# A cross-attention layer on one core: a new order of steps on all engines, values projected straight into the layout of the direct passes, and finer signals

## What is computed

```python
xn = _ln(x, ln1_w, ln1_b);  sx = _token_shift(xn, state[:, i1])
xxx = jnp.tanh((xn + sx * maa_x) @ maa_w1).reshape(b, l, 5, 1, EXTRA_MAA)
xxx = jnp.matmul(xxx, maa_w2).reshape(b, l, 5, E)
x5 = xn[:, :, None] + sx[:, :, None] * (maa_stack + xxx)          # five mixes
w = jnp.exp(-jnp.exp(time_decay + jnp.tanh(x5[:, :, 1] @ decay_w1) @ decay_w2))
r = x5[:, :, 3] @ Wr.T;  k = x5[:, :, 0] @ Wk.T;  v = x5[:, :, 2] @ Wv.T
g = jax.nn.silu(x5[:, :, 4] @ Wg.T)
def step(s, rkvw):                                                # scan over tokens, per head
    a = k_t[:, :, :, None] * v_t[:, :, None, :]
    out = jnp.einsum('bhk,bhkd->bhd', r_t, u * a + s)
    return (a + w_t[:, :, :, None] * s, out)
x = x + (head_norm(att) * gn_w + gn_b) * g @ Wo.T
xn2 = _ln(x, ln2_w, ln2_b);  sx2 = _token_shift(xn2, state[:, i0])
x = x + sigmoid(xr @ ffn_Wr.T) * (square(relu(xk @ ffn_Wk.T)) @ ffn_Wv.T)
```

## Time and profile before

| | us |
|---|---|
| median of 3 runs | 796.24 |
| the runs | 795.71, 796.24, 813.81 |
| span of the profiled execution | 793.8 |

### The profile page before, as it was taken

The page is one execution under the profiler, slowest core; times in us unless marked ns, Lnnn a source line. Parts: engine busy times, 40 slices in busy tenths (PEclk is TensorE's granted clock), DMA queues, the critical chain, the costliest instruction groups (busy, mean ns, idle before and its releaser), DMA issues.

```text
span 793.8 us, 17668 instructions
## 1 busy us (share of the span) xinstructions
PE 705.9 (89%) x7412; PEld 491.4 (62%) x7412; DVE 513.6 (65%) x767; ACT 324.7 (41%) x639; POOL 376.7 (47%) x223
## 2 busy tenths in 40 slices
PE   5986899997999889998799979998799978998797
PEld 4763677465674667556664665746665556755673
DVE  5638865695567774597556966677736965479441
...
DMA packets 19275, 28.79 MB, mean 36 GB/s; under 512 B 5888, under 2 KB 11776, under 8 KB 18176
## 3 DMA queue, kind: packets, MB, share of 16 engines
...
...
## 4 chain that ended last, share of the span: by engine, by line
PE 51%; issue 15%; POOL 14%; DVE 11%; ACT 7%; DMA 0%; POOLq 0%; DVEq 0%; ACTq 0%
PE FB L563 17%; PE BAB L820 7%; POOL pp L488 7%; PE FA L838 5%; PE FB L571 5%; PE FA L872 2%; ACT half L1048 2%; PE BAB L797 2%; PE FA L639 2%; DVE kvs L1357 2%; PE BAB L555 2%; PE FA L859 2%; PE BAB L733 2%; POOL mixes L453 2%; POOL mixes L451 1%
## 5 line engine op out<-in xcount | busy, mean ns | idle before, releaser
L488 POOL TENSOR_TENSOR pp<-rT,kT 128x2048 f32<-128x2048 f32 (+1 forms) x32 | 108.6, 3406 | 51.7 <-DVE rT L1229 51.7
L451 POOL TENSOR_TENSOR mixes<-mixes 128x1024 f32<-128x1024 f32 x30 | 72.0, 2400 | 127.9 <-ACT mixes L971 127.9
L453 POOL TENSOR_TENSOR mixes<-mixes,xnT 128x1024 f32<-128x1024 f32 x30 | 71.8, 2392 | 2.4
L563 PE MATMUL FB<-mixes,wk_s 128*128 128x256 f32 x256 | 66.1, 417 | 5.8 <-POOL mixes L453 3.5
L1321 DVE TENSOR_REDUCE half<-half 128x256 f32<-128x2048 f32 (+2 forms) x32 | 64.4, 2014 | 0.6
L504 POOL TENSOR_TENSOR acc<-acc,half 128x512 f32<-128x512 f32 x32 | 41.1, 1283 | 49.5 <-DVE half L1321 48.3
L563 PE MATMUL FB<-mixes,wv_s 128*128 128x256 f32 x256 | 60.8, 382 | 2.5 <-issue 1.5
L563 PE MATMUL FB<-mixes,wg_s 128*128 128x256 f32 x256 | 62.1, 392 | 0.0
L563 PEld LDWEIGHTS FB<-mixes,wk_s 128*128 128x128 f32 x256 | 52.1, 208 | 15.9 <-POOL mixes L453 4.5
L971 ACT ACTIVATE mixes<-FA,cols_s 128x256 f32<-128x256 f32 x116 | 45.4, 481 | 38.4 <-PE FA L639 33.4
L838 PE MATMUL FA<-wide,fk_s 128*128 128x256 f32 x256 | 57.2, 381 | 3.5 <-DVE wide L1472 2.2
...
## 6 DMA issues: line engine op xcount, KB each, us to landing
...
vp<-vT SPq DMA_DIRECT2D x128, 32.0 KB, 1.9
...
```

What stands on the lines that cost most here:

```text
L451: nc.gpsimd.tensor_tensor(slot, slot, sx, ALU.mult).then_inc(s_["mixm_ready"], 1)
L453: nc.gpsimd.tensor_tensor(slot, slot, xnT[:, :, 1:L + 1], ALU.add).then_inc(s_["mix_ready"], 1)
L488: ins = nc.gpsimd.tensor_tensor(pp[:, i % 2, 0:size].rearrange("p (n i j) -> p n i j", i=m, j=m), spread(r.unsqueeze(3), 3, m), spread(k.u ...
L563: ins = nc.tensor.matmul(dst[:, c * L:(c + 1) * L], weight[:, q, c * P:(c + 1) * P], src[:, q, :], start=(q == 0), stop=(q == C - 1))
```

## The change

1. **Order.** All lists of `ORDER` are new, and the pass without an `n_` step (front of 7, back of 6, tail of 5) gets a list of its own, `end`. The warm steps of the last pass are gone; `c_fv0` and `c_fv1` stand later there.
2. **Values.** `vT`, `prime` and its DMAs are gone. The centred weight `wv` is stored with its columns permuted (`f_centre`), so that the projection lands in grouped layout, and ACT copies it to `vp`. `b_vtok` turns `vp` with a strided output.
3. **Front banks.** `f_norm` waits for the first `c_mul` alone (in pass `end` for `relu` only), `c_fv1` now waits until ACT has read the norm from `FA` (`xnT_ready`), and `f_m20` waits for the second `c_mul`.
4. **Signals.** `f_norm`, `b_gn` and `b_norm2` signal their bank by halves; `ru_ready` comes before r is copied; `keys_ready` lets `b_ktok` start before the last decay of r; `kvfree_ready` lets `b_acc` start before DVE has added; `f_dec1` takes its mix by halves; `b_step` forms the totals before it waits for POOL.

```diff
@@ ORDER, tensor, last @@
-            c_fk b_score0 c_fr0 b_score1 c_fr1 b_g0 b_score2 b_g1 b_g2 b_score3 b_g3 c_fv0 b_score4 b_vtok c_fv1
-            b_ktok b_kv0 b_kv1 warm14 b_acc b_apply0 b_apply1 b_apply2 b_apply3 warm8 warm20 b_gn0 b_gn1 b_wo0
-            b_wo1 warm22 b_norm20 b_norm21 warm12""".split()),
+            c_fk b_score0 c_fr0 b_score1 c_fr1 b_g0 b_score2 b_g1 b_g2 b_score3 b_g3 b_score4 b_vtok b_ktok
+            b_kv0 b_kv1 c_fv0 b_acc b_apply0 b_apply1 b_apply2 b_apply3 c_fv1 b_gn0 b_gn1 b_wo0 b_wo1 b_norm20
+            b_norm21""".split()),
@@ walk @@
-            run(None, at(B - 1), at(B - 2), at(B - 3))
+            run(None, at(B - 1), at(B - 2), at(B - 3), order["end"])
@@ sync @@
-            def prime(b):
-
-                sp.wait_ge(s_["v_ready"], 2 * b + 2)
-                for c in range(C):
-                    for g in range(NG):
-                        sp.dma_start(vp[32 * c:32 * c + 32, g * L:(g + 1) * L], vT[32 * g:32 * g + 32, c * L:(c + 1) * L]
-                                     ).then_inc(s_["vp_ready"], 16)
@@ gpsimd @@
-                        pool.wait_ge(s_["r_ready"], 2 * b + 2)
+                        pool.wait_ge(s_["ru_ready"], 2 * b + 2)
@@ tensor @@
+            def transpose_grouped(dst, src):
+
+                eye = ident_s[:, :].rearrange("p (c i) -> p c i", c=C)
+                for t in range(T):
+                    for g in range(NG):
+                        to = dst[:, t * E:(t + 1) * E].rearrange("p (c g i) -> p g c i", c=C, g=NG)[:, g]
+                        ins = nc.tensor.transpose(to, src[:, g * L + t * P:g * L + (t + 1) * P], eye)
+                return ins
...
-                if not first(b):
-                    pe.wait_ge(s_["mixe_ready"], NMIX * b)
-                    pe.wait_ge(s_["mul_ready"], T * (b - 1))
-                transpose_channels(FA, xhat).then_inc(s_["xhatT_ready"], 1)
+                if isinstance(b, int) and b == 1:
+                    pe.wait_ge(s_["mixe_ready"], NMIX)
+                elif last(b):
+                    pe.wait_ge(s_["relu_ready"], 2 * b - 2)
+                elif not first(b):
+                    pe.wait_ge(s_["mul_ready"], T * b - 3)
+                transpose_channels(FA, xhat, range(T), s_["xhatT_ready"])
...
-                pe.wait_ge(s_["step_ready"], 4 * b + 4)
+                pe.wait_ge(s_["keys_ready"], b + 1)
...
-                pe.wait_ge(s_["kvs_ready"], b + 1)
+                pe.wait_ge(s_["kvfree_ready"], T * b + T)
...
+                        if q == 0 and not (isinstance(b, int) and b >= B - 2) and (t == 1 or isinstance(b, int) and b == B - 3):
+                            pe.wait_ge(s_["xnT_ready"], b + 3)
@@ scalar @@
-                act.wait_ge(s_["nrmT_ready"], T * b + T)
                 for c in range(C):
+                    act.wait_ge(s_["nrmT_ready"], 2 * b + 1 + c // 2)
...
-                copy = f_proj("projv_ready", vT, "v_ready", "q4_ready", 1, i)
+                copy = f_proj("projv_ready", vp, "v_ready", "q4_ready", 1, i)
@@ vector @@
-                        dve.wait_ge(s_["vp_ready"], 16 * NG * NG * (b + 1))
+                        dve.wait_ge(s_["v_ready"], 2 * b + 2)
...
             def f_centre(b, par, n):
-                centre(w_loaded["wv"], big["wv"][:, :, :].rearrange("p q (h s) -> p (q h) s", s=S),
-                       gT[:, 0:C * H], s_["vmean_ready"], s_["vcen_ready"])
+                mean = gT[:, 0:C * H]
+                centre(w_loaded["wv"], wv_raw.rearrange("p (h s) -> p h s", s=S), mean, s_["vmean_ready"])
+                nc.vector.tensor_scalar(mean, mean, 1.0 / S, None, ALU.mult).then_inc(s_["vmean_ready"], 1)
+                dve.wait_ge(s_["vmean_ready"], 2)
+                for q in range(C):
+                    own = slice(q * E, (q + 1) * E)
+                    ins = nc.vector.tensor_tensor(
+                        big["wv"][:, q, :].rearrange("p (g c h s) -> p c g h s", g=NG, c=C, s=S),
+                        wv_raw[:, own].rearrange("p (c g h s) -> p c g h s", c=C, g=NG, s=S),
+                        spread(mean[:, q * H:(q + 1) * H].rearrange("p (c g h) -> p c g h", c=C, g=NG).unsqueeze(4), 4, S),
+                        ALU.subtract)
+                ins.then_inc(s_["vcen_ready"], 1)
```

177 lines of the change are left out of this document (103 added, 74 removed).

## The result

The changed kernel takes **790.32 us** (median of 7 runs, 787.83 to 794.18) beside 797.5 us for the kernel before (7 runs, 795.71 to 813.81). The ratio is 0.993, 95% interval 0.991 to 0.995; the run of 813.81 us was in a slower state of the chip and is left out of it. The forecast was 770, with a range that began at 757 and ended at 790. So the kernel is faster, but by 0.7% and not by 3.3%, and the question is where the other 20 us went.

A forecast was written before the change was run, and what follows sets the result against it. Bound: PE's own queue and the back's chain, about equally late. Gains 17.0 (main passes) + 3.5 + 0 + 0.8 + 1.5 + 3.0 = 25.8 from 793.8 give 768.0; with 2.4 around the span, 770 us, range 757 to 790.

The forecast's parts named there:

- Start, to `f_lora0`: Main pass from `c_fk`: no new wait on the path, so `f_lora0` begins at 35.7 us, before 36.6.
- ACT takes it back: Main pass behind `f_lora0`: ACT's queue cuts the 0.9 us head start to 0.4; `f_k0` begins at 51.5.
- rival 3: PE falls to half clock in last pass and tail without warm steps: 776 us, or 779 with second pass; 14%.
- It just holds: Main pass: states are spread by 59.3 to 60.6 us, before the last apply at 60.8; applies end at 61.5.
- Root, late end: Main pass, applies to head norm: 5.2 or 7.2 us; the late end starts the norm at 68.7, pass 89.0.
- the pass of 87.0: Main pass takes 87.0 us, not 89.0, if the scan loses 1.9 wherever no POOL mix runs beside it.
- Pass `end`, 3.5: The pass before the last takes 89.6 us where it took 93.1: 3.5 won, bounds 0 to 6.
- Values 0: Removing the values' DMAs gains 0, since they landed before their first reader and cost nothing on the path.
- first and second pass (0.8 and 1.5): Gains of 0.8 us in the first pass (earlier first score) and 1.5 in the second (new order of scores).
- Last pass and tail, 3.0: Removing warm blocks wins 3.0 us there; bounds 6.6 won and 3 lost, with slow starts of 2.5 in two places.
- Rival 1: A new wait replaces the old ones in main passes, each winning only 1 us: 787 us; 20%.
- Rival 2: ACT's queue becomes the bound; a main pass takes 94.3 us, 11 lost, 807 in all; 6%.

The follow-up runs named there:

- e5: Changed kernel plus short strings of idle TensorE matmuls: 8 ahead of `f_m21`, 7 ahead of `b_gn0` in main passes, others in second and last pass; 773.99 us, ratio 0.971.
- e9: e5 with its 15 idle matmuls of a main pass cut from 128 columns to 4, same number and places; 782.24 us, ratio 0.978.
- e4: Changed kernel with POOL's `f_mix3` held until DVE's root is complete, in the main passes and pass `end`; 789.26 us, ratio 0.991.
- e13: e5 with the 7 idle matmuls ahead of `b_gn0` cut to 4 columns, the 8 ahead of `f_m21` whole; 774.66 us, ratio 0.972.
- e7: Changed kernel with POOL's `f_mix3` waiting for DVE's gate product in the main passes and `f_mix4` behind both `b_wo`; 783.2 us, ratio 0.986.
- e3: Changed kernel's code (values, signals) with all lists of steps of the kernel before; 795.59 us, ratio 0.998.
- e11: e5 without idle matmuls in the second pass and with the kernel before's lists in first and second pass; 776.56 us, ratio 0.974.
- e12: e7 plus idle TensorE matmuls, 8 ahead of `f_m21`, 2 ahead of `b_gn0`, and those of the last pass; 784.0 us, ratio 0.981.

## Why the prediction was wrong, point by point

- *The 2.4 us around the span.* 1.8 to 1.9 in every run that has both numbers; the 2.4 set the span of one run against the median of others.
- *Start, to `f_lora0`.* Right: 35.9 against 35.7, and 35.9 to 36.1 in every run with the new main list.
- *"ACT takes it back ... `f_k0` 51.5", and "PE waits here some 4 us in all".* The queue was right: at full clock (e5) `f_k0` begins at 51.2. **This is the step that failed, in what it left out.** I placed the waits and then priced every matmul behind them by rows at full clock. With 2.15 us of them in one piece the clock fell; `f_k0` came at 52.8. The prediction names it as what would make it wrong ("if the clock falls in the main passes, where the waits at `f_m21` to `f_k0` lie close together"), but gave it no price in the sum and no chance: rival 3 had the half clock in the last pass only. The main passes fell 16.3 us short of the sum (0.7 for 17.0): 13.0 by the clock (e9 against e5), 4.7 between the changed kernel and e9, of which some 2 are its pauses and the rest is open, less 1.4 by which the sum was too careful (443.8 and not 445.2).
- *Applies, "It just holds".* It holds, 61.6 in e5. Its terms add up to 58.3 to 60.1, not to 59.3 to 60.6; in the pass from 507.65 the spreading ended at 60.4 on DVE and 60.5 on ACT. The pauses, two of them, were in no term. Rows of before had them, with 7.8 us in three main passes, so the 92.4 that I subtracted from was itself not clean: its two passes without a pause took 91.9 and 91.8. Between clean passes the order gains 3.0 us, near the 3.4 of the sum.
- *Root, late end.* Right: 7.8 from the applies to `b_gn`, forecast 7.9. The stall of 2.2 moved to a later instruction, as the late end assumed; taking it out is worth 1.3 a pass by e4 and not 2.
- *`b_gn` to `wo` 2.8.* 3.9 measured, 2.8 in e5: the clock again.
- *The scan, and the pass of 87.0.* The prediction has 87.0 if the scan loses its 1.9 us. It lost them in all eight batches (2.29 us and not 4.15), with no mix of POOL beside it, and the pass was not shorter for it. The mix had moved to the spreading that follows, 5.87 us where it was 3.81, which has no term in the sum.
- *Pass `end`, 3.5.* 1.4 in the profiled run, 3.0 at full clock with a pause of 2.27 in it (e13), 5.1 in e7 with neither. The size was inside its bounds, 0 to 6.
- *Values 0.* Not contradicted: e3 has them and the signals together at 0.998 (0.995 to 1.002). The prices of first and second pass (0.8 and 1.5) had the wrong sign: `c_fk` came at 134.9 and 134.8 with the old lists (e3, e11), at 136.0 to 138.2 with the new ones (141.8 in e12), and at 138.0 to 141.9 where fillers stand in the second pass. Behind `wo` the new second list has `f_k3`, `f_m24`, `f_v2` and `f_v3` to do, 19.4 us to `c_fk` where it was 18.2. I had given that list its earlier scores and not counted what it puts behind `wo`. That is 1.2 of the 3.4; the other 2.2 are there when `wo` begins (118.8 and not 116.6), 0.8 of them at DVE's first product (52.03 and not 51.21), and no run looked for their cause.
- *Last pass and tail, 3.0.* 2.8, and the price of the missing warm matmuls is visible: `wo` took 8.52 us (7.11 before) behind a wait of 1.06, and `c_fk` 9.86 (7.07 before) behind one of 1.84. That is 4.2 together, near the 2.5 in each of two places, for which no row stood. With that price the low end is 6.6 - 5.0, so 1.6 won; the bound of 3 lost has no working. With short fillers in the last pass it is 95.7 to 98.1 in all kernels but one (e12, 99.3), 3 to 5 us better.
- *Rival 1* came out nearest in time (787), for another reason than its own: POOL left the scan and met the spreading and the root, and of the two only the root is a cost that a run showed (e4); most of the loss was the clock. *Rival 2* falls, by e5. *Rival 3* was right in mechanism and too narrow in place. The Trainium skill, "TensorE: Matmul & The Clock Gate", section "HAM oscillation — how this bites in real kernels", describes matmuls that start slow again behind each wait for a DMA. The trace agrees in kind, with 0.50 to 0.63 behind the waits of 2.1 to 2.2 us for `thR` in all five main passes, but not as a rule: in the first main pass of e7 the same wait (2.10) left `b_kv` at full clock, 2.02 us.
